# Two-layer attention with an adapter on one core: mask transposes, output product and key projection at other steps

## What is computed

```python
q, k, v = heads(x @ Wq), heads(x @ Wk), heads(x @ Wv)          # q, k turned by rope
w  = softmax(q k^T / sqrt(8) + mask)                            # mask (16, 1, 128, 128)
a_k, a_v = heads(adapter @ Wk), heads(adapter @ Wv)             # adapter (16, 128, 256)
out = w v + tanh(gate) * softmax(q a_k^T / sqrt(8)) a_v
x = layernorm(x + merge(out) @ Wo)
```

## Time and profile before

| | |
|---|---|
| time, median of 3 runs | 1206.8 us (1205.44 to 1206.95) |
| the profiled execution's own time | 1205.77 us |
| its span in the trace | 1204.0 us |
| PE busy | 1121.0 us, 93% |
| DVE busy | 956.0 us, 79% |
| ACT busy, POOL busy | 670.9 us (56%), 660.9 us (55%) |
| granted TensorE clock over the span | 0.981 of full |

### The profile page before, as it was taken

One profiled execution on the slowest core, in us unless ns is written; L12 is line 12 of the kernel. 1 busy time (PEld: TensorE's weight loads), 2 busy tenths in 40 slices (PEclk: granted clock), 3 DMA queues, 4 the chain that ended last, 5 costly groups with the idle time before them and its releaser, 6 DMA issues.

```text
span 1204.0 us, 30629 instructions
## 1 busy us (share of the span) xinstructions
PE 1121.0 (93%) x11732; PEld 924.7 (77%) x11732; DVE 956.0 (79%) x2219; ACT 670.9 (56%) x1703; POOL 660.9 (55%) x714
## 2 busy tenths in 40 slices
PE   5899998899899899888999999999999999999997
PEld 5677665566666666555799899999999999997887
DVE  6778877677778687786788888888888888877977
ACT  5466554577676676665455544444344434548663
POOL 4466555544455456244778655444544454837665
PEclk9899999899999899999999999999999999999999
DMA  5876443444443343421222000000000100101111
GB/s 160 207 182 149 115 121 105 112 111 114 116 123 111 110 124 105 112 64 43 84 71 72 1 1 1 1 1 2 1 1 1 36 1 1 36 19 36 36 36 36
DMA packets 107491, 83.05 MB, mean 69 GB/s; under 512 B 74172, under 2 KB 95804, under 8 KB 107346
## 3 DMA queue, kind: packets, MB, share of 16 engines
q1 hardware_dynamic: 107345, 81.10, 24.4%
HBM read 57.02 MB, written 23.07 MB: 67 GB/s over the span
## 4 chain that ended last, share of the span: by engine, by line
PE 65%; DVE 18%; issue 6%; SPq 4%; ACT 3%; DMA 2%; POOL 2%; POOLq 0%; DVEq 0%; ACTq 0%
PE bank L663 5%; PE bank L1632 5%; PE bank L1633 4%; PE bank L1634 4%; PE bank L1688 4%; PE bank L1661 4%; DVE B_nr L803 4%; SPq L1237 4%; PE bank L641 4%; PE bank L494 3%; PE bank L560 3%; PE bank L602 2%; PE bank L1648 2%; PE bank L495 2%; PE bank L496 2%
## 5 line engine op out<-in xcount | busy, mean ns | idle before, releaser
L1936 POOL TENSOR_TENSOR C_QK<-C_t1b,C_t2b 128x512 f32<-128x512 f32 x128 | 168.8, 1319 | 227.4 <-DVE C_t2b L1775 226.8
L1772 DVE SCALAR_TENSOR_TENSOR C_t1b<-bank,C_bcol,C_tabs 64x512 f32<-64x512 f32 x256 | 192.0, 750 | 38.3 <-PE bank L1634 34.2
L803 DVE TENSOR_REDUCE B_nr<-bank 128x4 f32<-128x512 f32 x256 | 164.4, 684 | 52.7 <-PE bank L602 52.1
L1062 ACT ACTIVATE PT<-bank 128x512 f32<-128x512 f32 x224 | 130.2, 597 | 106.4 <-PE bank L641 104.9
L1632 PE MATMUL bank<-C_XTh,C_Wh 128*128 128x512 f32 x256 | 112.2, 438 | 5.7 <-DVE C_XTl L1621 1.9
L1868 ACT ACTIVATE C_P<-bank,C_nm 128x128 f32<-128x128 f32 x256 | 90.5, 366 | 34.1 <-DVE C_nm L1785 32.4
L1887 ACT ACTIVATE C_V<-bank 128x512 f32<-128x512 f32 x64 | 38.0, 596 | 124.3 <-PE bank L1650 122.7
L1633 PE MATMUL bank<-C_XTl,C_Wh 128*128 128x512 f32 x256 | 101.6, 397 | 0.0
L1634 PE MATMUL bank<-C_XTh,C_Wl 128*128 128x512 f32 x256 | 101.3, 396 | 0.0
L663 PE MATMUL bank<-PT,vpool 128*32 128x128 f32 x2048 | 98.6, 289 | 2.0 <-ACT OTf L1072 2.0
L1775 DVE SCALAR_TENSOR_TENSOR C_t2b<-bank,C_bcol,C_tabs 128x512 f32<-128x512 f32 x128 | 96.1, 751 | 1.8
(11 more groups left out here) (271 smaller groups left out, 3578.8 us busy)
## 6 DMA issues: line engine op xcount, KB each, us to landing
Adrq<-PB SPq DMA_DIRECT2D x16, 192.0 KB, 3.0
Adrk<-PB SPq DMA_DIRECT2D x16, 192.0 KB, 3.1
stk<-Adrq SPq DMA_DIRECT2D x16, 192.0 KB
stk<-Adrk SPq DMA_DIRECT2D x16, 192.0 KB
Bdrq<-PB SPq DMA_DIRECT2D x16, 192.0 KB, 2.7
stk<-Bdrq SPq DMA_DIRECT2D x32, 96.0 KB
Bdrk<-PB SPq DMA_DIRECT2D x16, 192.0 KB, 2.8
stk<-Bdrk SPq DMA_DIRECT2D x32, 96.0 KB
```

The lines of the kernel that those rows point to most:

```text
L803: e.tensor_reduce(dst, bank[n % 2][:, :].rearrange("p (a b) -> p a b", a=4), AX.X, ALU.max, negate=True).then_inc(sem("m_dve"), 1)
L1062: e.activation(pt_of(n)[:, :], bank2(n)[:, :], ACT.Exp).then_inc(sem("e_act"), 1)
L1772: e.scalar_tensor_tensor(out=v4(t1b[kq][lo:lo + 64, :]), in0=v4(o[hi:hi + 64, :]), scalar=bc[hi:hi + 64, :], in1=tabsC[hi:hi + 64, 2 * kq ...
L1936: e.tensor_tensor(QK[v % 3][:, kq, :], t1b[kq][:, :], t2b[kq][:, :], ALU.add).then_inc(sem("rc_pool"), 1)
```

## The change

Four tables of step numbers change, and no work is added or left out.

- The key projection's first half of the pairs 10 to 15 is one step earlier (9 for 10, counted from `bg0(c)`), and all that hangs on it too. The new step is odd, so that the first half stands ahead of an even step's passes and the second half behind them.
- `mp`: for pair 9 three steps later (88 to 91), for the pairs 10 to 15 eleven steps later: from the step after `sh` and `to` (117, 149, ... 277) to an even step without other small products (128, 160, ... 288), which is step 0 of an item.
- `mask_t_out` of the pairs 10 to 15 is eight steps later, that of pair 9 two.
- `wo` of the items 17 to 26 is six steps later (140, 156, ... 284 to 146, 162, ... 290), from step 12 of an item to step 2 of the next; `tb` goes with it, from step 9 to step 15.

```diff
@@ -255,13 +255,13 @@
     xts = places((-1,), (-2, -4), (-2, 4), (-8, 8))
-    projs = places((2, 6), (2, 6, 10), (0, 10, 13), (-4, 10, 13))
+    projs = places((2, 6), (2, 6, 10), (0, 10, 13), (-4, 9, 13))
...
-    mask_turns = {s + (1 if c < 10 else 3): c for s, (c, _) in masked.items()}
-    masks_t_out = {bg0(c) + 28: c for c in range(8, 16)}
+    mask_turns = {s + (1 if c < 9 else 4 if c < 10 else 14): c for s, (c, _) in masked.items()}
+    masks_t_out = {bg0(c) + (28 if c < 9 else 30 if c < 10 else 36): c for c in range(8, 16)}
@@ -305,7 +305,7 @@
     def wo_step(g):
-        return to_step(g, 1) + (6 if g < 14 else 6 if g < 15 else 5 if g < 17 else 8 if g < 31 else 5)
+        return to_step(g, 1) + (6 if g < 14 else 6 if g < 15 else 5 if g < 17 else 14 if g < 27 else 8 if g < 31 else 5)
```

## The result

The changed kernel takes 1184.23 us (median of 4 runs, 1183.64 to 1186.67) beside 1206.12 us before (1202.08 to 1206.95): ratio 0.9829, 95% interval 0.9802 to 0.9855. The profiled execution took 1184.21 us, its span is 1182.4 us. The prediction said 1190, with 1182 to 1200.

The account below looks back on a forecast made before the run. PE, busy 93% of the span, was taken as the bound. The terms 7.8 + 3.7 - 1.5 - 2.4 + 1.1 + 1.0 + 7.3 = 17.0 us gave 1190 us, range for 8 in 10 1182 to 1200.

Parts of the forecast that it names:

- The wait: PE's idle time ahead of L543, pairs 10 to 15: gains 1.2 us at five sites, 1.8 at pair 10, together 7.8.
- the place of `mp`: Step 0 of an item: its 0.43 us fit into PE's 0.61 us wait for the maxima, so it costs nothing.
- The clock: Four slow stretches in the adapter block go once the waits of 1.6 us are gone: 7.3 us gained.
- The rival, that the clock doesn't come back: Adapter block: the four slow stretches have another cause and stay; gain only 8.7 us, 1198 us; chance 0.14.
- no window at 0.50 up to 500 us: Sign of being right: no stretch at half clock from 260 to 500 us in the profile after.
- a window at 0.50 within the block without a wait at L543: Sign of being wrong: half clock in the block though the L543 waits are gone, so the clock hangs on something else.
- `wo`: Moved from step 12 to step 2 of the next item: 0.36 us per even, 0.39 per odd item, 3.7 us gained.
- I give the two 0.35: Step 2, even items: loss per item from `residual` and statistics ahead of L803, and L836 inside POOL's new L776.
- `tb`: Moved from step 9 to 15 of an item: a loss of 0.15 us at ten items, 1.5 us, between 0 and 3.
- The key projection: Pairs 10 to 15: POOL's L1170 ends later, exponentials wait for ACT's second mask part; loss 0.4 us x 6, 2.4 us.
- Pair 9: `v` of step 89 gets the other bank: 1.1 us gained, plus 1.0 counted for the 10.2 us of low clock there.
- The other side's rival, more slow stretches than before: New waits of `v` for `divide`, up to ten sites, lower the clock: 1208 to 1218 us; chance 0.05.

Follow-up runs that it names:

- experiment 2: Kernel before with only `mp` and its DMAs at the steps of the change; ratio 0.9866 (0.9839 to 0.9893).
- experiment 8: Changed kernel with `mp` of pairs 10 to 15 at step 8 of the item instead of step 0 of the next; 1187.05 us, ratio 0.9869.
- experiment 12: Kernel before with `wo` of items 17 to 26 six steps later and `tb` left at its old step; ratio 0.9945 (0.9923 to 0.9968).
- e1: Kernel before with twelve more transposes of the identity ahead of `mp`'s wait in pairs 10 to 15; 1196.5 us, ratio 0.9939.
- e3: Kernel before with only `wo` and `tb` of items 17 to 26 six steps later; ratio 0.9940 (0.9913 to 0.9966).
- e4: Kernel before with only `mp` of pair 9 three steps later and its DMA two; ratio 0.9971 (0.9951 to 0.9991).
- e10: Kernel before with only the key projection one step earlier; ratio 1.0049 (1.0026 to 1.0073).
- experiment 5: Changed kernel with the key projection back at its old step; 1184.65 us, ratio 0.9852.
- experiment 7: Changed kernel with POOL's norm (L771, L776) of items 17 to 26 two steps later, behind L1165; 1181.53 us, ratio 0.9831.
- experiment 11: Changed kernel with PE waiting for ACT's copy of `sh` at the old place of `mp`, no work behind the wait; 1188.46 us, ratio 0.9883.
- experiment 6: Changed kernel with the adapter part's reciprocals in PSUM, so L836 has one input there instead of two in SBUF; 1183.66 us, ratio 0.9843.

## Why the prediction was right

**The wait and the place of `mp`.** Sized right: 1.2 us a pair in experiment 2, and `v` waits 0.47 us for `divide` at five sites where 0.5 to 0.8 was named. `mp` is hidden at step 0 as the prediction had it: the wait there is 0.17 us and not 0.61, and experiment 8 finds no time lost to it. At pair 10, for which 1.8 us were put, 1.5 came: from the L613 of step 116 to that of step 132 experiment 12, with the old order there and no slow stretch, takes 21.41 us (259.97 to 281.38), and experiment 2 takes 19.90 (255.41 to 275.31).

**The clock.** The term of 7.3 us, which no row could show ahead, held: no slow stretch from 240 to 490 us in the profile after, and e1 shows that it hangs on PE's idle time at this place and not on the moved work. Over all profiles: the five kernels with the old waits (before, e3, e4, e10, e12) have 30 of them and 15 slow stretches in the block, each starting within 2 us of such a wait; the eight without them have none. The mean granted clock was 0.989 over the 41 executions of these eight, and 0.982 over 64 of the kernel before. The rival, that the clock doesn't come back, falls. The page TensorE: Matmul & The Clock Gate of the Trainium skill, in Why this matters for your kernels, warns of longer idle gaps; here the clock fell behind 15 of 30 gaps of 1.6 us, and the measurement decides.

Two of the prediction's own signs went against it here. It named no window at 0.50 up to 500 us, and one starts at 497.43; and it named a window at 0.50 within the block without a wait at L543 as the sign that the clock hangs on something else. The 6.8 us at 497 is such a window, and the kernel before has others at 540 and 546. So waits at L543 were one cause in this block and not the only one. The stretch at 497 doesn't come with the change: e1 and e4, with the old order of `mp`, have one at the same steps (507.44 and 512.58). Ahead of it stand waits of 0.93 and 0.61 us at L560. All 14 profiles have these two waits, and six of them a slow stretch there.

**`wo`.** Right in kind, too small: 0.53 us each instead of 0.37 (experiment 12). The step that was off is that for even items "I give the two 0.35", for `residual` ahead of the maxima and for L836 inside POOL's new L776. By the distances from L613 to L613, experiment 12 gains 0.6 us at an even item (21.97 us from 431.27 to 453.24, against 22.57 from 440.47 to 463.04 before) and not 0.36, and 0.45 at an odd one (20.24 from there to 473.48, against 20.69 to 483.73) where 0.39 was put. L836 took 0.20 us there, in the middle of L776. The up to 0.9 us a site that the prediction names for contention with L776 did not come. The timelines of POOL and DVE after, even item:

```profile
401.42 1.23 POOL L776 TENSOR_SCALAR X<-z,mv,rstd 128x256 f32<-128x256 f32 x1
...
402.26 0.20 DVE L836 TENSOR_TENSOR rr<-rr,B_tg 128x36 f32<-128x36 f32 x1
```

**`tb`.** 1.5 us were put for it; it is 0.5 in all (experiment 12).

**The key projection.** Here the mechanism was wrong, and that its price fitted was luck. The late mask part on POOL makes nobody wait who matters: there is no wait of PE for ACT at L560 or L641 over 0.2 us after, and experiment 5 finds 0.1 us a pair where 0.4 stood. In its place there was a wait that the prediction did not have, L511 for `divide`, through L1165 behind the moved norm. The prediction named the norm's move and priced it at L836, when it should have asked what is queued behind it on POOL. It costs 0.4 us a pair (experiment 7), the same as the wrong term, so that the sum did not show the mistake.

**Pair 9.** The 1.1 us of the wait held: the L613 of step 100 comes 24.97 us behind the one before it in e1, with the old place of `mp` and no slow stretch, and 23.85 after. In the profiled execution all of the 10.2 us stretch went, which was worth 3.4 us (28.36 us before, less the 24.97) where 1.0 was put. That is partly luck, since the stretch comes back in some executions; the 3.5 us of experiment 4, for wait and clock together, have an interval that holds the 2.1 of the prediction too.

In all, a pair is 1.73 us shorter at full clock and not the 1.25 that the terms give (1.2 + 0.39 + 0.36 - 0.3 - 0.4). Over five and a half pairs this is 2.6 of the 4.6 us by which 17.0 was short of 21.6; pair 9 and the start-up are about 2.9, and the new slow stretch at 497 takes 1.2 back. Part of the 21.6 is the draw of this one pair of profiles, as the kernel before alone spreads over 12 us on one chip. The other side's rival, more slow stretches than before, had nothing: the new waits of 0.47 us left the clock alone in all kernels that have them.

Open is what it takes beside a wait to lower the clock. Half of the old waits of 1.6 us did, and none of the five of 1.5 us in experiment 11; these have the same place but `pv` behind them instead of `mp`. With an even chance each, five in a row without one come up once in 32, so this may be chance, and the lower mean clock of its other executions speaks for that. Four waits of 1.19 us at L511 in experiment 6 and five of 1.3 at L494 in experiment 10 left the clock alone in their profiles too.

## What to carry to other kernels

A bank or buffer given out by order of use ties a product to whatever stands ahead of it, and a moved step changes these ties for all that follow: print who last had the bank of each neighbour, as the key projection alone was 6 us slower by such a tie and free in company. Short waits of TensorE that repeat are worth more than their length where the clock falls behind them; filling one with useless matmuls tells the two prices apart in one run. When an instruction moves to another place on an engine, price first what is queued behind it there, and when one wait hides another, try the two cures together: alone they gave 0.03 and 0.4 us a pair here, together 1.15.

## What the runs showed of the hardware that was not expected

VectorE's L836 with two inputs in SBUF took 1.05 us inside GpSimd's TENSOR_TENSOR L459, ending with it, 0.20 us inside GpSimd's TENSOR_SCALAR L776, and 0.19 us inside L459 when one of its inputs was in PSUM (experiment 6). Counted over all 14 traces: started inside L459 it took 1.04 to 1.06 us all 60 times with both inputs in SBUF, and 0.19 to 0.20 all ten times with one in PSUM; started inside L776 it took 0.20 all 30 times, and inside L771, a TENSOR_TENSOR of one column, 0.20 all twelve times. The GPSIMD Engine Reference of the Trainium skill, section 1, names the contention for VectorE's instructions with two SBUF inputs; the runs agree for L459 (1.05 us against 0.20) and show none against the TENSOR_SCALAR (0.20 us), where the page makes no such difference. Why the TENSOR_SCALAR does not hold VectorE up is not shown.

TensorE's granted clock went to 1.2 GHz within 2 us of 15 of 30 waits of 1.6 us, for 3.4 to 6.8 us each, and stayed at 2.4 GHz in the same place when PE ran transposes of the identity during the wait, all six times (experiment 1). It fell also at a place where the waits before were only 0.93 and 0.61 us, in six of 14 profiles.
